# DVE's sum of a tile two units later, its statistics one unit later, and GpSimd's tile work in another order, in a language-model tower kernel

## Chip, cores and metric

The kernel runs on one core of a Trainium2 chip. The metric is the device time of one execution in microseconds (us). Of the kernel before there are three timed runs and one profiled execution. PE is the matrix engine (TensorE), PEld its weight loads, DVE is VectorE, ACT ScalarE, POOL GpSimd, SP the engine that issues plain DMAs.

## What is computed

Input are 8 sequences of 1024 tokens. Every token gets an embedding (three n-gram hashes, three gathered rows of 128, one projection). Then, with residual additions:

```
h = embed(x)                                    # 8 x 1024 x 128
y = layernorm(h)
for i in (cross, dot, cosine):                  # three attentions of width 128
    a_i = softmax(q_i k_i / s_i);  o_i = layernorm(a_i v_i) * g_i + b_i
gate = softmax([o_0, o_1, o_2] @ gw.T + gb)     # per token, 3 numbers
h = h + sum_i gate_i * o_i
y = layernorm(h);  p = softmax(y @ W_router + b_router)     # 32 experts
each expert takes its 256 most probable tokens (of 8192), applies up, silu, down
and adds p * result to h at those tokens
```

The cross attention has keys and values of half length (a convolution of stride 2). In the cosine attention q and k are divided by their norms.

## The kernel before

**Two blocks.** The first block does embedding, attention, gate and router probabilities, the second (`experts`) finds each expert's threshold bit by bit and runs the experts. The second starts when all engines have ended the first: the probabilities of the last tile are its input.

**Units and tiles.** A sequence has 8 tiles of 128 tokens. A *unit* is one tile and one attention branch, so there are 24 units in a sequence and N = 192 in all. Each engine's program (the functions under `block.tensor`, `block.vector`, `block.scalar`, `block.gpsimd`) runs one loop over `s`, 192 units and a tail of 14, written out, and each engine works through its own queue strictly in this order, with waits on semaphores. In unit `s` PE makes the scores of unit `s`, turns (transposes) the probs of `s-1` and multiplies `s-2` with the values. DVE evicts the output of `s-3` (`output`: `st` and `o`, L919 and L920), takes the row maxima of `s` (`maxima`, L913), ACT the exponent (L1078) and the copies of the turned probs into `pT` (L1087). A unit with `s % 3 == 0` is of the cross branch and has half the scores (the 512-wide maxima in the trace).

**Items.** Work for the coming sequences (gather and project tokens, keys, queries, values, the router) is cut into items, put by hand into the 24 slots of a sequence: the tables FIRST, SECOND (sequences 0 and 1), STEADY (2 to 6) and LAST (7), and DRAIN for the units after the last. Slot r of sequence b is unit 24b + r. In a slot's word, what stands before the bar is done by PE right after the scores, what stands behind it at the end of the unit; a plus means the sequence after, a minus the one before. The steady slots 14 to 16 put `v_cr` into the late part of 14 and the early part of 15, and the keys of the cosine branch, `k_c0+`, into 16. x2T (turned rows for the router) and route (router logits) are items too.

**Banks.** Items and turned probs share three PSUM banks. A little planner (before `build_program`) simulates unit times and deals the banks out; who uses a bank waits for the eviction of its last user (`release`).

**The end of a tile n** needs small steps on three engines, placed by unit:
- `tile_stats` (DVE, unit 3n+5), `tile_rstd` (POOL, 3n+5, L1187 to L1195), `tile_gate_logits` (DVE, 3n+6, L934 to L939), the exponent on ACT and `tile_gate` (DVE, 3n+7). Its last part is the chain u = h + sum over br of gate_r * o (three dependent additions, L956).
- `tile_sum` (POOL, 3n+8): z = the gated biases (L1201, L1205), then h1 = u + z (L1210), which needs DVE's chain.
- `tile_h1_stats` (DVE, 3n+9, L964 and L967), `tile_rstd2` (POOL, 3n+10, L1218 to L1223), `tile_x2` (ACT, 3n+11, L1100: the normalised row for the router).

`tile_gate` begins the chain with these lines, waiting for the buffer of two tiles before:

```
dve.wait_ge(gate_r_ok, n + 1)
if n >= 2:
    dve.wait_ge(h1_ok, n - 1)
```

**Other steps placed by unit.** DVE: `route_logits` (L858 to L863, an eviction), `route_probs` (L869 to L877) one or two units after the route item, `cos_scale` (L843 to L850: q and k times their inverse norms, two operations of 1024 columns) one unit before `k_c0`. POOL: `cos_norm` (L1177, L1180) two units before `k_c0`, `token_rstd` (L1168 to L1173), `gathers` (L1150, three indirect DMAs) four units before their gram item. In POOL's unit the order is tile_sum, tile_rstd, tile_rstd2, token_rstd and cos_norm, gathers.

Of the kernel before, what the change touches and what calls it, by code (L numbers as in the profile page):

```python
# [35 lines left out]
BR = 3  # L36
# [32 lines left out]
for _name, _width in (("ident", P), ("same", P), ("upto", P), ("after", P), ("pair", P), ("pair_below", P),  # L69
# [107 lines left out]
def build_program(nc, x_tok, emb, weights, cols, rows, consts, cand_bits, w_up, b_up, w_down, out):  # L177
    table = nc.dram_tensor("token_table", (TOK, XW), F32, kind="Internal").ap()
    with ExitStack() as ctx:
# [508 lines left out]
        def _(dve):  # L688
# [252 lines left out]
            def tile_gate(n):  # L941
# [6 lines left out]
                dve.tensor_scalar(gate[:, m, :], gate_e[:, m, :], gate_inv[:, m:m + 1], None, ALU.mult).then_inc(scale_ok, 1)  # L948
                dve.wait_ge(gate_r_ok, n + 1)
# [27 lines left out]
            for s in range(N + TAIL):  # L977
# [10 lines left out]
                if s % BR == 0 and 0 <= s - 9 < N:  # L988
                    tile_h1_stats((s - 9) // BR)
                if s % BR == 0 and 0 <= s - 6 < N:  # L990
                    tile_gate_logits((s - 6) // BR)
                if s % BR == 1 and 0 <= s - 7 < N:
                    tile_gate((s - 7) // BR)
                for where in range(2):
                    for k in PLACED.get((s - 1 - where, where), ()):
                        if ITEMS[k][0] == "route":
                            route_probs(*ITEMS[k][1:])
# [7 lines left out]
        def _(act):  # L1005
# [113 lines left out]
            for s in range(N + TAIL):  # L1119
# [8 lines left out]
                if s % BR == 2 and 0 <= s - 11 < N:  # L1128
                    tile_x2((s - 11) // BR)
# [11 lines left out]
                for k in items_at(s + 2):  # L1141
                    if ITEMS[k][0] == "xT":
                        normalise(*ITEMS[k][1:])


        @block.gpsimd
        def _(pool):
# [49 lines left out]
            def tile_sum(n):  # L1197

                m, t, b = n % 2, n % NT, n // NT
# [3 lines left out]
                for br in range(1, BR):  # L1203
                    pool.wait_ge(z_g, n * BR + br)
                    pool.tensor_tensor(zb[:, m, 0, :], zb[:, m, 0, :], zb[:, m, br, :], ALU.add).then_inc(z_g, 1)  # L1205
                pool.wait_ge(z_g, n * BR + BR)
# [44 lines left out]
            for s in range(N + TAIL):  # L1251
                if s % BR == 2 and 0 <= s - 8 < N:
                    tile_sum((s - 8) // BR)
                if s % BR == 2 and 0 <= s - 5 < N:
                    tile_rstd((s - 5) // BR)
                if s % BR == 1 and 0 <= s - 10 < N:
                    tile_rstd2((s - 10) // BR)
                for k in items_at(s + 2):
# [3 lines left out]
                    if name == "k_c" and j == 0:  # L1262
                        cos_norm(seq)
                for k in items_at(s + 4):
                    name, seq, j = ITEMS[k]
                    if name == "gram" and j < NT:
                        gathers(seq, j)

# [772 lines left out]
```

## Time and profile before

| | us |
|---|---|
| median of 3 runs | 1228.16 (1227.95 to 1229.41) |
| profiled execution | 1231.34 |
| its span, first to last instruction | 1229.6 |
| loop with full load | about 72 to 930 |
| second block from | 950.6 |

Over the span PE is busy 87%, DVE 68%, POOL 60%, ACT 55%, PEld 77%; the mean granted clock is 0.941 of full speed. The lines of a timeline give start and length in us, the engine, the line of the kernel, what is written from what, and in brackets how long the engine stood before it and which instruction ended that. A line of the waits gives who waited for whom, total us, times, and the longest. A number after x counts merged instructions.

### The profile page before, as it was taken

Reading aid. Unit: us, or ns where it says so; the run is one execution under the profiler, and the core shown is the slowest. Engines: PE = TensorE matmul, PEld = TensorE weight load, DVE = VectorE, ACT = ScalarE, POOL = GpSimd, SP = SyncE. Lnnn points to the kernel's source line nnn. Section 1 sums busy time; section 2 is a strip of 40 time slices with the busy share of each in tenths; the row PEclk is TensorE's granted clock in tenths of the full one; section 3 lists DMA queues with packets and bytes.
Section 4 is the critical chain, followed back from the end, with each engine's and each line's share of the span. In section 5 each row is a group of like instructions: output and inputs, shape, how many; then the busy total and the mean of one; then the engine's idle time right before and its main releaser. Section 6 shows DMA issues by size and latency. Waiting matters only on the chain. (4 is left out here: it accounts for less than half of the span.)

```text
span 1229.6 us, 23394 instructions
## 1 busy us (share of the span) xinstructions
PE 1065.2 (87%) x7550; PEld 944.5 (77%) x7550; DVE 830.4 (68%) x2686; ACT 677.6 (55%) x1742; POOL 736.0 (60%) x1200
## 2 busy tenths in 40 slices
PE   5689999999999999999999999999995357788672
PEld 4569888988988898998899899888884135666551
DVE  5346777787877778777777877787676777664220
ACT  0346756756676676666576666666663545434220
POOL 6356676677467547746864775353445027678885
PEclk9989999999999999999999999999997558889876
DMA  3011011010001001010100101000001103344442
GB/s 106 18 33 27 14 29 33 14 36 21 24 25 35 25 10 39 25 30 25 35 26 10 35 25 34 12 10 12 14 16 40 41 18 70 68 81 86 85 71 29
DMA packets 49085, 42.64 MB, mean 35 GB/s; under 512 B 6728, under 2 KB 44488, under 8 KB 48840
## 3 DMA queue, kind: packets, MB, share of 16 engines
q0 software_dynamic: 18432, 22.04, 9.5%
q1 hardware_dynamic: 30536, 19.13, 5.1%
q8 instruction: 62, 1.02, 0.3%
q14 instruction: 55, 0.45, 0.1%
HBM read 27.51 MB, written 13.63 MB: 33 GB/s over the span
## 5 line engine op out<-in xcount | busy, mean ns | idle before, releaser
L657 PE MATMUL mixed<-v,pT 128*128 128x131 f32 x2560 | 318.7, 276 | 3.6 <-DVE o L920 3.2
L657 PEld LDWEIGHTS mixed<-v,pT 128*128 128x128 f32 x2560 | 301.5, 190 | 5.0 <-issue 4.5
L913 DVE TENSOR_REDUCE neg_max<-scores 128x1 f32<-128x1024 f32 (+1 forms) x192 | 198.8, 1035 | 48.9 <-PE scores L444 48.8
L1150 POOL DMA_INDIRECT gram<-in_emb,ids x192 | 189.9, 989 | 64.9 <-issue 52.4
L1078 ACT ACTIVATE probs<-scores,neg_max 128x1024 f32<-128x1024 f32 (+1 forms) x192 | 186.2, 970 | 38.8 <-DVE neg_max L913 38.3
L1087 ACT ACTIVATE pT<-turned 128x512 f32<-128x512 f32 x219 | 130.0, 593 | 74.8 <-PE turned L638 73.9
L1201 POOL TENSOR_TENSOR zb<-row,gate 128x384 f32<-128x384 f32 x64 | 54.5, 851 | 144.2 <-DVE gate L948 143.8
L638 PE MATMUL turned<-con,probs 128*128 128x128 f32 x876 | 126.7, 275 | 7.6 <-ACT probs L1078 3.5
L1977 POOL DMA_INDIRECT out_h<-yw,slots x64 | 102.4, 1601 | 36.1 <-issue 20.6
L638 PEld LDWEIGHTS turned<-con,probs 128*128 128x128 f32 x876 | 101.6, 141 | 22.3 <-ACT probs L1078 8.9
L1968 POOL DMA_INDIRECT xg<-token_table,slots x64 | 64.5, 1008 | 67.6 <-DVE slots L1799 49.0
L919 DVE BATCH_NORM_STATS2 st<-mixed 128x6 f32<-128x128 f32 x192 | 56.1, 292 | 59.3 <-PE mixed L657 57.7
L442 PE MATMUL scores<-k_hi,xT_hi 128*128 128x512 f32 x192 | 82.2, 428 | 0.3 <-DVE k_lo L818 0.3
L956 DVE SCALAR_TENSOR_TENSOR u<-o,gate_r,u 128x128 f32<-128x128 f32 x128 | 78.2, 611 | 4.5
L1087 ACT ACTIVATE pT<-mixed 128x512 f32<-128x512 f32 x101 | 60.0, 594 | 30.5 <-PE mixed L638 30.0
L1908 ACT ACTIVATE hid<-scores,bup 114x256 f32<-114x256 f32 (+1 forms) x96 | 38.4, 471 | 69.3 <-PE scores L1614 69.2
L443 PE MATMUL scores<-k_lo,xT_hi 128*128 128x512 f32 x192 | 75.8, 395 | 0.0
L444 PE MATMUL scores<-k_hi,xT_lo 128*128 128x512 f32 x192 | 75.8, 395 | 0.0
L1629 PE MATMUL mixed<-wd,hid 114*128 114x128 f32 x384 | 61.4, 321 | 9.4 <-issue 9.4
L1218 POOL TENSOR_SCALAR shift<-mv 128x1 f32<-128x1 f32 x64 | 14.6, 229 | 89.4 <-DVE mv L967 87.4
L1205 POOL TENSOR_TENSOR zb<-zb 128x128 f32<-128x128 f32 x128 | 60.6, 474 | 10.0
L1629 PEld LDWEIGHTS mixed<-wd,hid 114*128 114x128 f32 x384 | 55.7, 228 | 12.5 <-issue 12.0
(350 smaller groups left out, 2550.2 us busy)
## 6 DMA issues: line engine op xcount, KB each, us to landing
wd<-in_w_down SPq DMA_DIRECT2D x32, 171.0 KB
token_table<-w SPq DMA_DIRECT2D x16, 320.0 KB, 2.4
out_h<-h SPq DMA_DIRECT2D x16, 256.0 KB, 2.3
gram<-in_emb,ids POOLq DMA_INDIRECT x192, 2.5
wu<-in_w_up SPq DMA_DIRECT2D x8, 170.5 KB, 4.0
w<-in_weights SPq DMA_DIRECT2D x1, 1174.0 KB, 6.4
xg<-token_table,slots POOLq DMA_INDIRECT x64, 3.1
out_h<-yw,slots POOLq DMA_INDIRECT x64
```

The lines of the kernel that those rows point to most:

```text
L442: pe.matmul(dst, lhs[0], rhs[0], start=first_one, stop=False)
L443: pe.matmul(dst, lhs[0], rhs[1], start=False, stop=False)
L444: return pe.matmul(dst, lhs[1], rhs[0], start=False, stop=last_one)
L638: last = pe.transpose(dst[:, j * P:(j + 1) * P], probs[:, n % 2, half * 512 + j * P:half * 512 + (j + 1) * P], ident)
L657: last = pe.matmul(mixed[:, 0:C + 3], pT[:, n % 2, j * P:(j + 1) * P], vals[:, 0:C + 3], start=(j == 0), stop=(last_half and j == half * 4 ...
L913: dve.tensor_reduce(neg_max[:, n % 4:n % 4 + 1], scores[:, (n % 2) * S:(n % 2) * S + width], AX_X, ALU.max, negate=True).then_inc(maxed, 1)
L956: last = dve.scalar_tensor_tensor(out=u[:, m, br, :], in0=o[:, n % 4, br, 0:C], scalar=gate_r[:, m, br:br + 1], in1=u[:, m, br - 1, :] if ...
L1078: act.activation(probs[:, n % 2, 0:width], scores[:, (n % 2) * S:(n % 2) * S + width], ACT.Exp, bias=neg_max[:, n % 4:n % 4 + 1], accum_ou ...
L1087: act.activation(pT[:, n % 2, half * 512:half * 512 + 512], shared_bank(TURNED_ON[n, half]), ACT.Identity).then_inc(pT_ok, 1)
L1150: pool.indirect_dma_start(gram[:, t % 4, g, :], None, emb[g], bass.IndirectOffsetOnAxis(ap=ids[:, s, t, g:g + 1], axis=0)).then_inc(gather ...
L1629: last = pe.matmul(down_bank[:, half * C:(half + 1) * C], hid[:, e % 2, c, half * P:(half + 1) * P], wd[:, e % EB, c, :], start=(c == 0), ...
L1977: pool.indirect_dma_start(rows_out, bass.IndirectOffsetOnAxis(ap=slots[:, k:k + 1], axis=0), yw[:, e % EB, half, :], None, compute_op=ALU. ...
```

## The change

Four edits.
1. DVE: the chain leaves `tile_gate` and becomes `tile_chain`, in unit 3n+9, after the gate logits of the next tile. `tile_h1_stats` moves from 3n+9 to 3n+10, behind `tile_gate`.
2. POOL: `tile_sum` keeps z; the addition becomes `tile_add` in unit 3n+9. In a unit token_rstd and cos_norm come first, then tile_rstd, tile_sum, tile_add, gathers, and tile_rstd2 last.
3. ACT: `tile_x2` goes from the start to the end of its unit, except in the units after the last.
4. The router's items stand one to three slots later, in SECOND and STEADY (and so LAST). With that the planner deals some banks otherwise.

```diff
--- before.py
+++ after.py
@@ -89,12 +89,12 @@
          "v_cr1+ | v_dc1+", "k_c0+ | gram2++", "k_c1+ | v_dc2+ v_dc3+", "x2T0 q_c0+ | v_dc4+ gram3++",
          "route0 | v_dc5+ gram4++")
 SECOND = ("v_dc6 | v_dc7", "| gram5+", "| q_c1", "xT0+ |", "gram6+ | v_dc0+", "k_d0+ | v_dc1+",
-          "gram7+ | v_dc2+", "qk_raw0+ | v_dc3+", "| gram8+", "x2T1- | qk_raw1+", "| route1-", "| gram0++", "xT1+ |",
+          "gram7+ | v_dc2+", "qk_raw0+ | v_dc3+", "| gram8+", "| qk_raw1+", "x2T1- |", "| route1- gram0++", "xT1+ |",
           "k_d1+ | qk_raw2+", "down0+ | qk_raw3+", "k_cr0+ | gram1++", "| v_cr0+", "| gram2++",
           "k_c0+ | v_cr1+", "k_c1+ | v_dc4+", "q_c0+ | gram3++", "gram4++ | v_dc5+", "x2T0 | v_dc6+", "gram5++ v_dc7+ | route0")
 STEADY = ("| xT0+", "q_c1 | ", "k_d0+ | v_dc0+", "gram6+ | v_dc1+", "qk_raw0+ | v_dc2+", "gram7+ | v_dc3+",
-          "qk_raw1+ |", "gram8+ |", "|", "x2T1- |", "xT1+ | route1-", "k_d1+ | qk_raw2+", "down0+ | qk_raw3+",
-          "k_cr0+ | ", "| v_cr0+", "v_cr1+ | gram0++", "k_c0+ | gram1++", "k_c1+ | v_dc4+", "q_c0+ | gram2++",
+          "qk_raw1+ |", "gram8+ |", "|", "|", "xT1+ | x2T1-", "k_d1+ | qk_raw2+", "down0+ | qk_raw3+",
+          "k_cr0+ | route1-", "| v_cr0+", "v_cr1+ | gram0++", "k_c0+ | gram1++", "k_c1+ | v_dc4+", "q_c0+ | gram2++",
           "gram3++ | v_dc5+", "gram4++ | v_dc6+", "x2T0 | v_dc7+", "gram5++ | route0", "|")
 
 LAST = tuple(line + extra for line, extra in zip(STEADY, ("",) * 4 + (" probT0", "", " probT1", "", " probT2") + ("",) * 15))
@@ -946,6 +946,9 @@
                 dve.scalar_tensor_tensor(out=gate_r[:, m, :], in0=gate_e[:, m, :], scalar=gate_inv[:, m:m + 1],
                                          in1=rstd[:, m, :], op0=ALU.mult, op1=ALU.mult).then_inc(gate_r_ok, 1)
                 dve.tensor_scalar(gate[:, m, :], gate_e[:, m, :], gate_inv[:, m:m + 1], None, ALU.mult).then_inc(scale_ok, 1)
+
+            def tile_chain(n):
+                m = n % 2
                 dve.wait_ge(gate_r_ok, n + 1)
                 if n >= 2:
                     dve.wait_ge(h1_ok, n - 1)
@@ -985,12 +988,14 @@
                     maxima(s)
                 for k in PLACED.get((s, 0), ()):
                     evict(k)
-                if s % BR == 0 and 0 <= s - 9 < N:
-                    tile_h1_stats((s - 9) // BR)
                 if s % BR == 0 and 0 <= s - 6 < N:
                     tile_gate_logits((s - 6) // BR)
+                if s % BR == 0 and 0 <= s - 9 < N:
+                    tile_chain((s - 9) // BR)
                 if s % BR == 1 and 0 <= s - 7 < N:
                     tile_gate((s - 7) // BR)
+                if s % BR == 1 and 0 <= s - 10 < N:
+                    tile_h1_stats((s - 10) // BR)
                 for where in range(2):
                     for k in PLACED.get((s - 1 - where, where), ()):
                         if ITEMS[k][0] == "route":
@@ -1125,7 +1130,7 @@
                     for k in PLACED.get((s - 1 - where, where), ()):
                         if ITEMS[k][0] == "route":
                             route_exp(*ITEMS[k][1:])
-                if s % BR == 2 and 0 <= s - 11 < N:
+                if s % BR == 2 and N <= s < N + 11:
                     tile_x2((s - 11) // BR)
                 for k in PLACED.get((s, 0), ()):
                     evict(k)
@@ -1141,6 +1146,8 @@
                 for k in items_at(s + 2):
                     if ITEMS[k][0] == "xT":
                         normalise(*ITEMS[k][1:])
+                if s % BR == 2 and 11 <= s < N:
+                    tile_x2((s - 11) // BR)
 
 
         @block.gpsimd
@@ -1196,13 +1203,16 @@
 
             def tile_sum(n):
 
-                m, t, b = n % 2, n % NT, n // NT
+                m = n % 2
                 pool.wait_ge(scale_ok, n + 1)
                 pool.tensor_tensor(zb[:, m, :, :], R("ln_b").rearrange("p (i c) -> p i c", c=C),
                                    gate[:, m, :].unsqueeze(2).to_broadcast([P, BR, C]), ALU.mult).then_inc(z_g, 1)
                 for br in range(1, BR):
                     pool.wait_ge(z_g, n * BR + br)
                     pool.tensor_tensor(zb[:, m, 0, :], zb[:, m, 0, :], zb[:, m, br, :], ALU.add).then_inc(z_g, 1)
+            def tile_add(n):
+
+                m, t, b = n % 2, n % NT, n // NT
                 pool.wait_ge(z_g, n * BR + BR)
                 pool.wait_ge(u_ok, n + 1)
                 if t % 4 == 0 and b > 0:
@@ -1249,22 +1259,24 @@
                     if ITEMS[k][0] == "gram":
                         gathers(*ITEMS[k][1:])
             for s in range(N + TAIL):
-                if s % BR == 2 and 0 <= s - 8 < N:
-                    tile_sum((s - 8) // BR)
-                if s % BR == 2 and 0 <= s - 5 < N:
-                    tile_rstd((s - 5) // BR)
-                if s % BR == 1 and 0 <= s - 10 < N:
-                    tile_rstd2((s - 10) // BR)
                 for k in items_at(s + 2):
                     name, seq, j = ITEMS[k]
                     if name == "xT":
                         token_rstd(seq, j)
                     if name == "k_c" and j == 0:
                         cos_norm(seq)
+                if s % BR == 2 and 0 <= s - 5 < N:
+                    tile_rstd((s - 5) // BR)
+                if s % BR == 2 and 0 <= s - 8 < N:
+                    tile_sum((s - 8) // BR)
+                if s % BR == 0 and 0 <= s - 9 < N:
+                    tile_add((s - 9) // BR)
                 for k in items_at(s + 4):
                     name, seq, j = ITEMS[k]
                     if name == "gram" and j < NT:
                         gathers(seq, j)
+                if s % BR == 1 and 0 <= s - 10 < N:
+                    tile_rstd2((s - 10) // BR)
 
         first_part.__exit__(None, None, None)
         attn.close()
```

## Rows read from the trace of the kernel before

**Rows 1.** Windows: stretch, busy us of PE, PEld, DVE, ACT, POOL; clock, DMA.
```profile
400.00:500.00 100.00, 97.83 (x726) 89.69 (x725) 75.33 (x224) 64.62 (x166) 62.61 (x114) 1.00 0.10 28
```

**Rows 2.** Waits of PE, 150 to 870 us: total us, times, longest.
```profile
PE mixed L657 <- DVE o L920: 2.6, 5, 0.5
PE turned L638 <- ACT probs L1078: 2.0, 4, 0.6
PE turned L442 <- ACT pT L1087: 1.8, 3, 0.6
PE mixed L638 <- ACT probs L1078: 1.7, 3, 0.9
PE mixed L442 <- ACT pT L1087: 0.6, 1, 0.6
```

**Rows 3.** Timeline of PE: start, length, instruction, idle time before it.
```profile
272.33 0.66 PE L638 MATMUL turned<-con,probs 128*128 128x128 f32 x4 [0.84 <-DVE h L833]
...
298.17 0.66 PE L638 MATMUL turned<-con,probs 128*128 128x128 f32 x4 [1.16 <-DVE v L823]
...
483.99 2.02 PE L657 MATMUL mixed<-v,pT 128*128 128x131 f32 x16 [0.52 <-DVE o L920]
...
506.74 0.60 PE L564 MATMUL turned<-con,w 128*128 128x128 f32 x4
```

**Rows 4.** Timeline of DVE, units of slots 12, 15 and 16.
```profile
467.72 0.28 DVE L869 TENSOR_REDUCE r_sum<-wide 128x4 f32<-128x128 f32 x1
...
468.70 0.29 DVE L919 BATCH_NORM_STATS2 st<-mixed 128x6 f32<-128x128 f32 x1
...
478.94 0.14 DVE L934 TENSOR_TENSOR logit<-o,rstd 128x9 f32<-128x9 f32 x1
...
480.45 0.25 DVE L843 RECIPROCAL inv_norm<-norm 128x16 f32<-128x16 f32 x1 [0.98 <-POOL norm L1180]
...
483.37 0.28 DVE L919 BATCH_NORM_STATS2 st<-mixed 128x6 f32<-128x128 f32 x1
```

**Rows 5.** Timeline of POOL, slots 14 and 15, and one gather.
```profile
475.24 0.19 POOL L1187 TENSOR_TENSOR sum_sq<-exp_sum 128x3 f32<-128x3 f32 x1
...
477.04 2.92 POOL L1177 TENSOR_TENSOR norm<-norm,p_half 128x16 f32<-128x16 f32 x1
480.12 0.29 POOL L1180 TENSOR_SCALAR norm<-norm 128x16 f32<-128x16 f32 x1 [0.16 <-POOL norm L1177]
...
483.44 0.94 POOL L1150 DMA_INDIRECT gram<-in_emb,ids  x1 [0.30 <-issue]
```

**Rows 6.** Timeline of DVE: the last two additions, two tiles.
```profile
457.73 1.34 DVE L956 SCALAR_TENSOR_TENSOR u<-o,gate_r,u 128x128 f32<-128x128 f32 x2
...
502.27 0.74 DVE L956 SCALAR_TENSOR_TENSOR u<-o,gate_r,u 128x128 f32<-128x128 f32 x2
```

**Rows 7.** Timeline of ACT: slots 13, 17 and 20.
```profile
473.96 0.20 ACT L1024 ACTIVATION_READ_ACCUMULATOR xn<-qk_raw 128x1 f32 x1
...
489.67 0.49 ACT L1100 ACTIVATE w<-h,shift,rstd 128x128 f32<-128x128 f32 x1 [2.13 <-POOL shift L1223]
...
506.22 0.59 ACT L1087 ACTIVATE pT<-turned 128x512 f32<-128x512 f32 x1
```

**Rows 8.** Timeline of DVE after the last product.
```profile
937.36 0.30 DVE L928 BATCH_NORM_AGGREGATE mv<-st 128x2 f32<-128x6 f32 x3
...
939.57 0.17 DVE L934 TENSOR_TENSOR logit<-o,rstd 128x9 f32<-128x9 f32 x1 [1.22 <-POOL rstd L1195]
...
943.73 0.29 DVE L964 BATCH_NORM_STATS2 st<-h 128x6 f32<-128x128 f32 x1 [0.95 <-POOL h L1210]
...
944.78 0.26 DVE L858 TENSOR_TENSOR wide<-mixed,row 128x96 f32<-128x96 f32 x1 [0.48 <-PE mixed L570]
```

**Rows 9.** Timeline of PE and ACT after the last product.
```profile
941.74 0.88 PE L564 MATMUL turned<-con,w 128*128 128x128 f32 x3 [4.61 <-ACT w L1100]
...
945.87 0.49 ACT L1100 ACTIVATE w<-h,shift,rstd 128x128 f32<-128x128 f32 x1
```

## Prediction, made before the result was known

> **What bounds the kernel now.** I read the busy time by windows first. In a window of the loop the matrix engine is busy 97.8 of 100 us, DVE 75, ACT 65, POOL 63, at the full granted clock, 2.4 GHz [rows 1]. What DVE can gain is thus worth only what it takes from the 2.2 us of every 100 in which PE stands. Then the waits of PE name those 2.2 us [rows 2]: 2.6 us for `o` (five times 0.52), 2.4 us (1.8 and 0.6) for a pT copy, 3.7 us (2.0 and 1.7) for a probs. The timeline places them: the wait for `o` is in slot 16 of sequences 2 to 6, the pT waits in slot 17 (four times 0.6), the waits for probs in slot 0 and in the last sequence. Two more, in sequence 1, wait for `h` and `v` of DVE, 0.84 and 1.16 us [rows 3]. Nothing else in the loop is open to a gain. After the last product, whose statistics DVE aggregates at 937.36 [rows 8], the order is another: the tail of tile 63 is one serial chain of DVE, POOL, ACT and PE, and every microsecond in it is one of the time.
>
> The profiled execution took 1231.34 us (span 1229.6), 3.2 us above the median 1228.16; the sum is made against it and carried to the median.
>
> **Slots 15 and 16, the largest term.** Today DVE ends slot 15 with the scaling of q and k: logits from 478.94, a wait of 0.98 us for POOL's norm, scaling from 480.45, next `st` at 483.37, so 2.92 us of scaling [rows 4]. PE's product waits for the `o` just behind it, 0.52 us [rows 3]. The change puts into that same unit, ahead of the scaling, two more things: the chain of three additions (slot 15 is a multiple of 3) and `route_probs`, since route1 now stands second in slot 13 and its probabilities come two units later.
> - POOL: the norm now stands before the tile's rstd. It can start when the last square is read, 474.16 [rows 7], and takes 477.04 to 480.41, 3.37 us; the rstd takes 475.24 to 477.04, 1.8 us [rows 5]. The moved statistics of the tile before come first: DVE's would be ready about 473.1 by its place in slot 13, and from such statistics to the x2 that needs POOL's four pass some 1.5 us (943.73 + 0.6 to 945.87 [rows 8, 9]). So the norm starts at 474.6, ends at 478.0, and rstd is there at 479.8 instead of 477.0. DVE, at the logits today at 478.94, now stands for it.
> - DVE from 479.8: logits 0.5, chain, `route_probs` 0.98 (467.72 to 468.70), scaling 2.92 [rows 4].
> - The chain's first addition starts 0.37 us before the second; the other two take 1.34 us in the one tile and 0.74 in the other [rows 6]: 1.7 or 1.1 us. POOL forms z right after rstd, so here I take the slow one.
> The end is 479.8 + 0.5 + 1.7 + 0.98 + 2.92 = 485.9, 2.5 us later than 483.37. But x2T and route leave slots 9 and 10, 0.4 and 0.8 us of PE work, and return only in slots 10 and 13, so PE and what follows it (squares, keys) run 0.8 us early up to slot 13: 1.8 us remain, all on PE, since `o` is what it waits for already. Bounds: 1.2 with the fast chain, 2.5 without the early slots; 0.5 less than nothing if the gap closed. Taken 1.8, five sequences: **+9.0**.
>
> What decides between 1.7 and 1.1 for a chain is who reads beside it: both tiles' rows have the same operands [rows 6]. The Trainium skill ("SBUF — State Buffer", Who interferes with whom) says that a DVE instruction with two SBUF inputs is shut out while a GpSimd instruction that reads SBUF holds the shared port, for the whole of it. By that rule a chain that z no longer accompanies costs 1.1 everywhere; were POOL done with z when the chain starts in slot 15, the sum would be 3.0 us lower.
>
> **Slot 17, a gain.** ACT stands 2.13 us at 489.67 for POOL's shift, with k_hi and a pT behind it [rows 7]; x2 moves to the end of the unit, behind both, and PE's 0.6 us go. Four times: **-2.4**. What is late next is that same x2: POOL's shift now stands behind the gathers of slots 14, 15 and 16 (three each, 0.94 + 0.30 us [rows 5]), at about 494.5 to 495 by adding them up from rstd; ACT reaches x2 about 494 and holds q_hi and the next pT for some 0.8 us, of which PE has 0.5 in hand: 0.3 us, five times, **+1.5** (from 0 to 1.5 us each).
>
> **Slot 0, a gain.** DVE's maximum of slot 23 comes late because the chain stands in slot 22. It loses 1.7 and gets 0.5 of statistics. All waits for probs, 3.7 us [rows 2]: **-3.7**.
>
> **Sequence 1.** The 0.84 us for `h` follow a slowed scaling with z beside it, which is now elsewhere; at 298.17 the planner gives the transposes another bank, freed by gram5 and not by v_dc7, one eviction and 0.9 us earlier [rows 3]. **-1.8**, from 0 to -2.5.
>
> **Slot 21, a new wait.** x2T0 is PE's first item there, at 506.74 [rows 3], and needs the x2 of unit 20. x2 was the first thing of ACT's unit 20 and is now the last, after the pT at 506.22 + 0.59 [rows 7]; its 0.49 us end at 507.2. PE stands 0.5 us, in six sequences (2 to 7): **+3.0** (0 to 0.6 each).
>
> **After the last product.** Statistics of DVE are there at 937.66, POOL's rstd today only at 939.5, because z of tile 62 stood before it [rows 8]. With the new order: rstd 938.9, logits 0.6, then the chain of tile 62, 1.7, ahead of gate 63 (941.7), then the statistics of 62 to 942.3, POOL's four of them to 943.8 and only then z of 63, because POOL's queue has them in this order; x2 of 62 at 944.3. From x2T (941.74 [rows 9]) to DVE's route logits (944.78 [rows 8]) are 3.0 us, now 944.35 to 947.4; the statistics of tile 63 stand behind this eviction (0.8 us), at 948.2 instead of 943.73. Everything after, x2 at 945.87 [rows 9] first, moves by that: **+4.4**. Low bound 1 (rstd earlier, only the queue of POOL counts), high 5.5.
>
> Edits at nothing: the gate stays where it is, `tile_add` is POOL's own successor of z and its buffer is written two tiles later; the other maxima wait for their scores, as the idle 25 us of DVE in 100 show [rows 1]. If that cover went, 1.1 us a tile would show.
>
> **Sum:** 9.0 - 2.4 + 1.5 - 3.7 - 1.8 + 3.0 + 4.4 = +10.0 us: 1241.3 in a profile like this one, **1238.2** as median. From the bounds of its terms it lies between 1231 and 1245.
>
> **Rivals.** (a) Faster. The norm, now first on POOL, is there before DVE needs it, so the 0.98 us wait of slot 15 pays for the chain. That decides if rstd comes by 478.5, for which the squares would have to come 1.3 us early, not 0.8; and if z is over. Then slot 16's 2.6 us go too: -2.6 - 2.4 - 3.7 - 1.8 + 4.4 - (nothing at slot 21) = -6.1, 1222.0. For it speaks that DVE's work is spread better over the three units; against it, that slot 15 holds three long pieces. Chance 0.13. The Trainium skill ("Perfetto Trace Analysis", Identifying the Most-Contended Engine) holds the matmul share to be a bad measure of headroom and the weight loads' share a good one; that is 89.7 here and would leave room for more than 2.2 us in 100, but the trace has no wait behind it.
> (b) No change. The overrun of slot 15 is half (0.9 x 5), slot 21 and the end too (1.5 and 2.2), the gains whole: +4.5 - 7.9 + 1.5 + 2.2 = +0.3, 1228.5. Chance 0.10.
> (c) Worse. POOL, with the norm, the rstd, z and nine gathers in three units, is so late that x2 holds ACT 1.5 us in slot 18, not 0.3: +6.0 more, 1244, and up to 1248. Against it: PE is itself later by then. Chance 0.15.
> My forecast keeps 0.62.
>
> **Chances.** 0.2%, 2.5 us, is about what a measurement here tells from no change. Slower by more than that: the forecast, (c): 0.77. Within: (b), 0.10. Faster: (a), 0.13. The range 1227.5 to 1246 leaves out (a) and the top of (c).
>
> **What would show it.** Right: PE's wait for `o` in slot 16 grows from 0.5 to 2 us and more, DVE's wait on POOL's rstd appears in slot 15, that for the norm vanishes; the waits at slots 0 and 17 vanish; PE waits for ACT's x2 0.5 us in slot 21; the second block starts over 4 us later after the last product. Wrong: `o` waits of 0.5 us or less in slot 16, no wait at slot 21, or statistics of tile 63 within 8 us of the last product's end.

## The result, and the profile after

The changed kernel takes **1241.71 us** (median of 4 runs, 1240.82 to 1245.38), the kernel before 1228.06 on the same chip: a ratio of 1.0114 (95% interval 1.0094 to 1.0135), slower. The profiled execution took 1240.82 us, span 1239.0, 9.5 us over that of before. The forecast was 1241.3 in a profile like that and 1238.2 as a median.

Where the 9.5 us lie, from the starts of PE's scores in the two traces (before, after, in us): up to the first unit 2.6 less; sequence 0, 115.6 and 114.3; **sequence 1, 112.8 and 118.2**; sequence 2, 109.0 and 110.7; sequences 3 to 5, 109.3 and 109.5 on average; sequence 6, 103.7 and 104.7; sequence 7, 95.9 and 95.3; **from the last product to the second block, 13.7 and 19.0**; the second block 0.1 more. Sequences 3 to 5 thus pay almost nothing, against all that the forecast puts there. The median moved more than the traces, by 13.65 us: the profiled execution of the changed kernel was the fastest of its four, that of the kernel before slower than all four runs of it.

PE's waits between 150 and 870 us of the changed kernel, the view of [rows 2]:

```profile
PE turned L558 <- DVE qk_raw L850: 5.6, 3, 2.0
PE mixed L558 <- DVE qk_raw L850: 3.3, 2, 1.7
PE mixed L657 <- DVE o L920: 2.4, 5, 0.5
PE turned L638 <- DVE h L833: 2.1, 1, 2.1
PE turned L638 <- ACT pT L1092: 1.8, 1, 1.8
PE mixed L564 <- ACT w L1105: 1.5, 3, 0.7
```

Five waits for the scaling of q and k (8.9 us) stand in slot 16, where the kernel before had one of 0.2 us; the waits for `o` stay at 0.5 us each; the waits for probs and those of slot 17 are gone. PE is busy 97.29 of the 100 us from 400, where it was 97.8 [rows 1].

Slot 15 on DVE, the answer to [rows 4], and POOL beside it [rows 5]:

```profile
480.87 0.79 DVE L934 TENSOR_TENSOR logit<-o,rstd 128x9 f32<-128x9 f32 x1 [0.46 <-POOL rstd L1202]
...
481.97 0.35 DVE L959 SCALAR_TENSOR_TENSOR u<-o,gate_r,h 128x128 f32<-128x128 f32 x1
482.36 0.88 DVE L959 SCALAR_TENSOR_TENSOR u<-o,gate_r,u 128x128 f32<-128x128 f32 x2
483.15 0.28 DVE L869 TENSOR_REDUCE r_sum<-wide 128x4 f32<-128x128 f32 x1
...
484.09 0.24 DVE L843 RECIPROCAL inv_norm<-norm 128x16 f32<-128x16 f32 x1
...
486.91 0.29 DVE L919 BATCH_NORM_STATS2 st<-mixed 128x6 f32<-128x128 f32 x1
```
```profile
475.69 2.91 POOL L1184 TENSOR_TENSOR norm<-norm,p_half 128x16 f32<-128x16 f32 x1
...
479.95 0.88 POOL L1202 TENSOR_TENSOR rstd<-var_eps,m_half 128x3 f32<-128x3 f32 x1
480.80 0.83 POOL L1208 TENSOR_TENSOR zb<-row,gate 128x384 f32<-128x384 f32 x1
```

The norm is over at 479.0, and DVE stands for rstd, which POOL forms behind it. Then come logits (1.10 us up to the chain), chain (1.18), probabilities (0.94) and scaling (2.82): 6.0 us in a row. PE stands 1.66 us at the turning of the keys (`k_c0+`, the first item of slot 16, which reads the scaled rows) and 0.47 us for `o` at the product behind it, where it stood 0.52 in all [rows 3]:

```profile
486.01 0.63 PE L558 MATMUL turned<-con,qk_raw 128*128 128x128 f32 x4 [1.66 <-DVE qk_raw L850]
...
487.54 2.03 PE L657 MATMUL mixed<-v,pT 128*128 128x131 f32 x16 [0.47 <-DVE o L920]
```

Two things were not foreseen. The first is in sequence 1, on POOL and on ACT, and then on PE (units 26 and 27):

```profile
188.06 0.46 POOL L1220 TENSOR_TENSOR h<-u,zb 128x128 f32<-128x128 f32 x1 [5.50 <-DVE u L959]
188.75 1.09 POOL L1157 DMA_INDIRECT gram<-in_emb,ids  x1 [0.24 <-issue]
...
192.43 0.23 POOL L1175 TENSOR_SCALAR shift<-mv 128x4 f32<-128x4 f32 x1
```
```profile
194.40 0.88 ACT L1097 ACTIVATE xn<-h,shift,rstd 128x128 f32<-128x128 f32 x2 [2.42 <-POOL shift L1180]
```
```profile
196.85 0.66 PE L558 MATMUL mixed<-con,qk_raw 128*128 128x128 f32 x4 [1.09 <-DVE h L833]
...
200.46 0.63 PE L638 MATMUL turned<-con,probs 128*128 128x128 f32 x4 [1.80 <-ACT pT L1092]
202.03 0.87 PE L638 MATMUL mixed<-con,probs 128*128 128x128 f32 x4 [0.94 <-DVE q_lo L813]
```

POOL's addition waits in its queue 5.5 us for a chain that now comes two units later; the gathers and the tokens' statistics stand behind it. Later in the same sequence, in unit 42, PE stands 2.09 us for `h`. x2, now ahead of the copy of gramT on ACT, waits for POOL's shift, and POOL is late because two small operations take 0.99 and 1.06 us beside DVE's scaling (268.29 to 270.57), for 0.23 and 0.21 us elsewhere:

```profile
268.62 0.99 POOL L1228 TENSOR_SCALAR shift<-mv 128x1 f32<-128x1 f32 x1
269.67 1.06 POOL L1229 TENSOR_SCALAR ve<-mv 128x1 f32<-128x1 f32 x1
```
```profile
271.69 0.49 ACT L1105 ACTIVATE w<-h,shift,rstd 128x128 f32<-128x128 f32 x1 [2.14 <-POOL shift L1233]
```

The second is PE's clock. Windows of the changed kernel (length, PE's busy time, granted clock, DMA share, GB/s): behind the stall of sequence 1, in slot 16 of sequence 2, and in slot 16 of sequence 3.

```profile
202.00:205.00 3.00, 2.97 (x15) 0.55 0.19 46
...
375.00:380.00 5.00, 4.53 (x25) 0.66 0.23 59
```
```profile
486.00:489.00 3.00, 2.52 (x21) 1.00 0.23 57
```

Three times in the loop, from 202.3, 274.0 and 376.4 us, the clock is granted at half, 1.2 GHz, for 3.4 us; in the trace of before it is at 2.4 GHz in all three places. Slots 16 of sequences 2 and 3 have the same 1.66 + 0.47 us of stall and last 9.23 and 7.62 us: **1.6 us for one such stretch**. At that price the three make some 4.8 of the 9.5 us, an estimate from this one pair.

### The profile page after: what moved, and what is told of

Same layout as the page of the kernel before. It is cut to its first block and busy times, and to the rows that moved or that the text cites. A ratio compares the mean times of both kernels' runs of the same rounds, so it can differ in the third digit from the quotient of the medians.

```text
span 1239.0 us, 23392 instructions
## 1 busy us (share of the span) xinstructions
PE 1062.0 (86%) x7548; PEld 944.8 (76%) x7550; DVE 816.0 (66%) x2686; ACT 671.7 (54%) x1742; POOL 728.3 (59%) x1200
## 5 line engine op out<-in xcount | busy, mean ns | idle before, releaser
L657 PE MATMUL mixed<-v,pT 128*128 128x131 f32 x2560 | 322.5, 278 | 3.0 <-DVE o L920 3.0
L657 PEld LDWEIGHTS mixed<-v,pT 128*128 128x128 f32 x2560 | 305.2, 192 | 4.2 <-issue 4.2
L1092 ACT ACTIVATE pT<-turned 128x512 f32<-128x512 f32 x212 | 126.0, 595 | 63.0 <-PE turned L638 62.8
L638 PE MATMUL turned<-con,probs 128*128 128x128 f32 x848 | 120.8, 274 | 6.7 <-DVE h L833 2.1
L638 PEld LDWEIGHTS turned<-con,probs 128*128 128x128 f32 x848 | 98.1, 141 | 19.2 <-ACT probs L1083 9.7
L1220 POOL TENSOR_TENSOR h<-u,zb 128x128 f32<-128x128 f32 x64 | 29.9, 466 | 110.9 <-DVE u L959 88.6
L1092 ACT ACTIVATE pT<-mixed 128x512 f32<-128x512 f32 x108 | 64.4, 596 | 47.9 <-PE mixed L638 47.8
L638 PE MATMUL mixed<-con,probs 128*128 128x128 f32 x432 | 65.4, 274 | 1.4 <-DVE q_lo L813 0.9
L1874 ACT ACTIVATE below_a<-odd,cand 128x448 bf16<-128x448 f32 x58 | 38.8, 669 | 44.6 <-DVE cand L1720 42.9
```

The costliest lines, as they stand in the source:

```text
L638: last = pe.transpose(dst[:, j * P:(j + 1) * P], probs[:, n % 2, half * 512 + j * P:half * 512 + (j + 1) * P], ident)
L657: last = pe.matmul(mixed[:, 0:C + 3], pT[:, n % 2, j * P:(j + 1) * P], vals[:, 0:C + 3], start=(j == 0), stop=(last_half and j == half * 4 ...
L1092: act.activation(pT[:, n % 2, half * 512:half * 512 + 512], shared_bank(TURNED_ON[n, half]), ACT.Identity).then_inc(pT_ok, 1)
```

## The experiments

The runs come in three groups, each on a chip of its own, with the kernel before run beside it; its median is given with the group, and a ratio is to that median. The changed kernel itself was not run again in any group.

### First group: one part of the loss at a time (before: 1229.79 us)

**u_chain14.** The chain of slot 15 alone goes one unit forward.

```diff
+                if s % UNITS == 14 and s < N:
+                    tile_chain((s - 8) // BR)
-                if s % BR == 0 and 0 <= s - 9 < N:
+                if s % BR == 0 and s % UNITS != 15 and 0 <= s - 9 < N:
                     tile_chain((s - 9) // BR)
```

> The changed kernel with one edit: in slot 15 alone the chain of three additions is issued one unit earlier (slot 14), so slot 15 holds logits, route_probs and the scaling, without the chain. Theory (the chain is the larger part of slot 15's overrun): PE's gaps in slot 16 fall from 2.1 us to 0.5 to 1.0 us in each of five sequences, and no half-clock stretch follows there; time 6 to 8 us lower, 1234 to 1236. Rival (POOL's rstd, now behind the norm, sets DVE's time in slot 15): DVE waits 1.5 us or more for rstd instead of 0.46, the gaps shrink by 0.5 us at most, time at most 3 us lower, 1239 or more.

Measured: 1238.96 us, ratio 1.0065 (1.0042 to 1.0087). Slot 16 and slot 18 on PE, and ACT ahead of the latter:

```profile
484.53 0.63 PE L558 MATMUL turned<-con,qk_raw 128*128 128x128 f32 x4 [0.54 <-DVE qk_raw L850]
```
```profile
497.40 0.38 PE L506 MATMUL turned<-w,gramT 128*128 128x128 f32 x1 [0.54 <-ACT pT L1094]
```
```profile
495.89 0.49 ACT L1107 ACTIVATE w<-h,shift,rstd 128x128 f32<-128x128 f32 x1 [2.25 <-POOL shift L1235]
```

The gap falls by 1.1 us, as much as the chain takes; DVE's wait for rstd stays at 0.46 us. The half-clock stretch of sequence 2 is gone. Half of it comes back in slot 18: PE, now earlier, meets the pT held by the late x2. So the theory has the mechanism right. The ratio is 0.5 points under the changed kernel's 1.0114, some 6 us and so the low end of the 6 to 8 us expected; the time itself is 3 us above the forecast.

**u_addlast.** POOL adds behind the gathers of its unit.

```diff
-                if s % BR == 0 and 0 <= s - 9 < N:
-                    tile_add((s - 9) // BR)
                 for k in items_at(s + 4):
...
                         gathers(seq, j)
+                if s % BR == 0 and 0 <= s - 9 < N:
+                    tile_add((s - 9) // BR)
```

> The changed kernel with one edit: POOL's addition u + z of a tile is issued behind the gathers of its unit instead of before them. Theory (in sequence 1 POOL stands 5.5 us for DVE's u with gathers and the tokens' statistics queued behind, and this makes PE's stalls of 1.1, 1.8 and 0.9 us in units 26 and 27 and the half-clock stretch behind them): those stalls fall to below 1.0 us in sum, sequence 1 is 3 to 5 us shorter, 1237 to 1239. Rival (the stalls come from DVE's own place of the work, not from POOL's queue): sequence 1 as before the edit within 1 us, 1241 to 1242.

Measured: 1245.11 us, ratio 1.0109 (1.0076 to 1.0142). Sequence 1 is 114.0 us instead of 118.2, the 1.1 us gap of unit 26 and the half-clock stretch of unit 27 gone, 1.5 us of the others left (the kernel before has 1.1 there): this shows the cause of 4.2 of the 5.4 us of sequence 1. Unit 42 keeps its 2.09 us and its stretch. The time is not lower for other reasons. Slot 20 of sequence 0 is 1.5 us longer (the addition behind three gathers lets DVE wait 1.35 us with its statistics, and the scaling of q and k stands behind them, so PE waits 1.55 us for 0.95); sequence 5 has a half-clock stretch; and the trace reached the first unit 2.6 us later than the changed kernel's.

```profile
168.34 0.63 PE L558 MATMUL mixed<-con,qk_raw 128*128 128x128 f32 x4 [1.55 <-DVE qk_raw L850]
```

**u_drain.** The tail in the old order from unit 193. The edit also puts the statistics ahead of the gate in their unit all through the loop, which the forecast below leaves out.

```diff
+                if s % BR == 0 and s > N and s - 9 < N:
+                    tile_h1_stats((s - 9) // BR)
                 if s % BR == 0 and 0 <= s - 6 < N:
                     tile_gate_logits((s - 6) // BR)
-                if s % BR == 0 and 0 <= s - 9 < N:
+                if s % BR == 0 and 0 <= s - 9 and s <= N:
                     tile_chain((s - 9) // BR)
+                if s % BR == 1 and 0 <= s - 10 and s <= N + 1:
+                    tile_h1_stats((s - 10) // BR)
                 if s % BR == 1 and 0 <= s - 7 < N:
                     tile_gate((s - 7) // BR)
-                if s % BR == 1 and 0 <= s - 10 < N:
-                    tile_h1_stats((s - 10) // BR)
+                    if s > N:
+                        tile_chain((s - 7) // BR)
...
                     tile_sum((s - 8) // BR)
-                if s % BR == 0 and 0 <= s - 9 < N:
+                    if s > N:
+                        tile_add((s - 8) // BR)
+                if s % BR == 0 and 0 <= s - 9 and s <= N:
                     tile_add((s - 9) // BR)
```

> The changed kernel with one edit: from unit 193 on (the tail after the last scores) the chain stands again behind its gate, the statistics of a tile one unit earlier and POOL adds behind its z; the rstd stays ahead of z. Theory (the serial tail pays for the moved chain and statistics): from the last product to the second block 18.97 us become 12 to 14, nothing else moves, time 5 to 7 us lower, 1235 to 1237. Rival (the tail is set by route and x2T of the last tiles, not by chain and statistics): 17 us or more stay, time within 2 us of the changed kernel's.

Measured: 1236.49 us, ratio 1.0050 (1.0036 to 1.0065), but the tail takes 16.15 us, not 12 to 14; the rest came from the loop, and in this trace 1.5 us from an earlier first unit. In the loop the earlier statistics bring POOL's queue (rstd2, norm, rstd) forward, DVE no longer stands at the logits, and slot 16's gap is 1.2 us in three sequences instead of 1.66 (1.8 and 1.5 in sequences 5 and 6):

```profile
476.76 0.79 DVE L934 TENSOR_TENSOR logit<-o,rstd 128x9 f32<-128x9 f32 x1
```

So what sets the start of slot 15's work is a queue that begins with the statistics two units before. And with no wait for rstd at all a gap of 1.2 us stays: that much goes with the serial work on DVE.

**u_dve_pool.** Chain, statistics and POOL's order as before; x2 at the end and the items in their new slots remain.

> The changed kernel with DVE's chain and statistics and POOL's order put back as in the kernel before; left are x2 at the end of its unit and the router's items in their new slots. Theory (the loss is in the chain's and POOL's part): 1225 to 1229, that is the kernel before, plus 0.5 us in slot 21 of six sequences, less 0.6 us in slot 17 of four and 1 us in unit 47. Rival (the late x2 holds ACT and then PE): 1231 to 1235, with waits of PE for x2 in slot 21 of 1 us or for pT in slots 18 and 19.

Measured: 1233.98 us, ratio 1.0034 (1.0020 to 1.0049): the rival, though its wait in slot 21 is 0.7 us and not 1. A steady sequence is 0.5 to 1.0 us longer than before: slot 17's gap is gone, but x2T waits for x2 in slot 21, and slot 9, from which x2T has left, shows a wait for probs that it used to cover.

```profile
503.92 0.30 PE L564 MATMUL turned<-con,w 128*128 128x128 f32 x1 [0.71 <-ACT w L1100]
```
```profile
555.80 0.44 PE L638 MATMUL turned<-con,probs 128*128 128x128 f32 x2 [0.50 <-ACT probs L1078]
```

### Second group: the clock, x2's place, and a mended version (before: 1229.07 us)

**b_stall.** The kernel before, with DVE made late in slot 15.

```diff
+        pad_v = asb("pad_v", [P, 8, 8, BR])
...
                     if name == "k_c" and j == 0:
+                        if seq > 2:
+                            for j2 in range({3: 4, 4: 5, 5: 6, 6: 7, 7: 8}[seq]):
+                                dve.tensor_reduce(pad_v[:, seq, j2, :], gain[:], AX_X, ALU.add)
                         cos_scale(seq)
```

> The kernel before with dummy reductions (128x393 each, into a scratch tile) on DVE ahead of the scaling of q and k in slot 15 of sequences 2 to 6: 4, 5, 6, 7 and 8 of them. They make PE's stall in slot 16 longer, about 1.2 us in sequence 2 up to 3 us in sequence 6, and nothing else of the change is there. Theory (the granted clock halves for 3.4 us in a loop that is otherwise full when PE stands some 1.7 us or more, and that costs 1.6 us on top): half-clock stretches behind the long stalls of the later sequences, none behind the first, and those slots longer by the stall and 1.6 us. Rival (the half-clock stretches of the changed kernel come from elsewhere): no stretch behind any of them, each slot longer by its stall alone.

Measured: 1233.85 us, ratio 1.0043 (1.0026 to 1.0060). The waits for the scaling are 0.71, 1.10, 1.27, 2.05 and 2.51 us in sequences 2 to 6. Windows around the last two (PE, PEld, DVE, ACT, POOL, then the clock):

```profile
698.00:708.00 10.00, 7.47 (x59) 6.91 (x59) 9.61 (x25) 4.71 (x9) 8.02 (x11) 1.00 0.15 39
809.00:819.00 10.00, 7.75 (x49) 7.12 (x50) 9.39 (x22) 4.14 (x8) 3.72 (x8) 0.83 0.09 28
```

The stall of 2.51 us is followed by half clock and its sequence is 3.6 us longer; that of 2.05 us is not, and its sequence is 0.95 us longer. One stretch thus follows a stall alone, with nothing else of the change there; it is one case, and the theory's 1.7 us is not a boundary, since 2.05 us had none. And in sequence 3 slot 16 is 1.25 us longer but slot 17 **0.85 shorter** with x2 at its old place (its pT is ready once PE is late); the added stall costs 0.4 us. So slot 17's gap can be had only once, by x2's new place or by being late.

**u_x2.** The changed kernel with x2 at the start of its unit.

```diff
-                if s % BR == 2 and N <= s < N + 11:
+                if s % BR == 2 and 0 <= s - 11 < N:
                     tile_x2((s - 11) // BR)
...
-                if s % BR == 2 and 11 <= s < N:
-                    tile_x2((s - 11) // BR)
```

> The changed kernel with x2 at the start of its unit on ACT, as before. Theory (the later statistics and POOL's order make x2's shift come late in slot 17, about 4 us after ACT would ask for it, with k_hi and pT behind it): the 0.41 us gaps of slot 21 go, but PE stands 2 to 4 us more in slot 17 or 18, time 1250 to 1262; x2's new place is then a condition of the other edits. Rival (x2 at the start finds its shift ready as before but for slot 17's old 0.6 us): 1240 to 1243.

Measured: 1265.76 us, ratio 1.0287 (1.0259 to 1.0316). ACT stands 5.14 us for the shift, PE 3.58 in slot 17: the theory, at a time 4 us above its range. x2's new place is a condition of the rest.

```profile
507.24 0.49 ACT L1105 ACTIVATE w<-h,shift,rstd 128x128 f32<-128x128 f32 x1 [5.14 <-POOL shift L1231]
```

**c14_drain_x2late.** u_chain14, u_drain (with its earlier statistics in the whole loop) with POOL's old order in the tail too, and x2 of slot 17 one unit later. The lines for the last:

```diff
-                if s % BR == 2 and 11 <= s < N:
+                if s % BR == 2 and 11 <= s < N and s % UNITS != 17:
                     tile_x2((s - 11) // BR)
+                if s % UNITS == 18 and s < N:
+                    tile_x2((s - 12) // BR)
```

> The changed kernel with three edits together: slot 15's chain in slot 14; the tail (from unit 193) in the order of the kernel before on DVE and POOL, statistics of a tile ahead of the gate of their unit; and the x2 of slot 17 issued at the end of unit 18 instead of unit 17. Theory (in slot 18 ACT stands for POOL's shift with the pT behind it, 0.54 us of PE once slot 16 is mended, and the same wait holds gramT in unit 42): the slot 18 gaps of 0.54 us and most of the 2.1 us of unit 42 go with its half-clock stretch, the tail is back at 13.7 us, time 1226 to 1230. Rival (the late x2 comes late for something else): a gap of over 0.5 us at x2T in slots 21 or 10, or a POOL wait for x2, time 1231 to 1234.

Measured: 1227.21 us, ratio 0.9981 (0.9967 to 0.9996). Slot 18's gap and 1.5 of the 2.1 us of unit 42 are gone, with its half-clock stretch, but slots 20 and 21 of that sequence are 0.7 us longer each. Sequences 2 to 5 last 107.8 to 108.9 us, where the kernel before has 109.0 to 109.4. The tail is at 15.1 us. What the earlier statistics give in it was not taken apart.

**best1.** The same with x2T0 in the second half of its unit (`"| x2T0 v_dc7+"`) and POOL's addition behind the gathers in sequence 1 alone.

> The one before with two more edits: x2T of slot 21 in the second half of its unit, and in sequence 1 alone POOL's addition behind the gathers. Theory (the 0.41 us of slot 21 and the stalls and half-clock stretch of units 26 and 27 are the last losses of the change): 6 x 0.4 and 4 us lower than the one before, 1220 to 1224, faster than both kernels. Rival (x2T in the second half delays the router's item and route's probabilities, the bank of the planner moves and a pT waits): no lower than the one before less 4.

Measured: **1220.56 us, ratio 0.9928 (0.9901 to 0.9955)**, with no half-clock stretch in the loop past the first units, like the kernel before. From 400 to 500 us (the sum row of that window):

```profile
sum 100.00, PE 99.25 PEld 91.50 DVE 77.33 ACT 66.34 POOL 65.64; mean PE 99.25 PEld 91.50 DVE 77.33 ACT 66.34 POOL 65.64
```

PE is at 99.25 of 100, and sequences 2 to 7 are 1.4 to 2.0 us shorter each than before.

### Third group (before: 1248.07 us)

This chip runs the kernel before itself 19 us slower, and in three of the four traces engines stand for releasers that the trace can't name ("remote"), which no other trace shows between 100 and 900 us. These four traces also lack the landings of the gathers, which all others have, so part of it can be a hole of the trace. One in best2:

```profile
500.57 0.60 ACT L1019 ACTIVATE k_hi<-mixed 128x512 fp32r<-128x512 f32 x1 [3.87 <-remote]
```

Only local readings are taken from it. The changed kernel was not run on this chip, so how much of a loss here is the edit's and how much the chip's can't be told from the ratio.

**u_pool.** POOL's order as before, the addition ahead of rstd.

> The changed kernel with POOL's order as before (z first, then rstd, then the tile's second rstd, then the tokens' statistics, the norm and the gathers); the addition stands in its new unit, behind z. Theory (in slot 15 DVE stands for rstd because the norm was put ahead of it, and in unit 42 ACT stands for a shift queued behind gathers): PE's gap of 1.66 us in slot 16 falls to 0.5 to 1.0 us in each of five sequences and the 2.1 us of unit 42 to about 1 us, with their half-clock stretches gone; time 1232 to 1236. Rival (POOL's second rstd now waits in its unit for the statistics of DVE, with the norm and the gathers behind it, and the norm comes later than DVE wants it): DVE stands for the norm in slot 15, the gap stays at 1.5 us or more, time 1240 to 1246.

Measured: 1305.18 us, ratio 1.0446 (1.0397 to 1.0495). Each had a part. Slot 16's gap falls to 0.4 us in sequences 2 to 4 and 0.74 in the next two, as in the theory. But, as in the rival, POOL asks for the statistics ahead of DVE's issue of them and stands up to 6.4 us, rstd and the tokens' statistics behind it, and PE pays in other slots: against the changed kernel's trace slot 0 is 2.2 to 4.0 and slot 10 2.2 to 3.9 us longer in each of sequences 2 to 6.

```profile
482.40 0.24 POOL L1228 TENSOR_SCALAR shift<-mv 128x1 f32<-128x1 f32 x1 [4.07 <-DVE mv L970]
```
```profile
521.64 0.63 PE L558 MATMUL turned<-con,qk_raw 128*128 128x128 f32 x4 [0.43 <-DVE qk_raw L850]
```

POOL's new order is thus needed by the later statistics, though slot 16 alone is better off with the old one.

**u_tables.** The router's items in their old slots.

> The changed kernel with the router's items in their old slots (x2T1 first in slot 9, route1 second in slot 10), so its probabilities leave slot 15. Theory (route_probs is 1 us of slot 15's overrun, and the late x2 makes x2T1 wait): the gap of slot 16 falls from 1.66 to about 0.7 us, a new gap of some 0.5 us stands at x2T1 in slot 9, time 2 to 4 us lower, 1238 to 1240. Rival (POOL's rstd and the chain set slot 15, and probabilities only fill a wait): the slot 16 gap over 1.3 us, time 1242 to 1245.

Measured: 1297.81 us, ratio 1.0384 (1.0337 to 1.0432). In slot 9 PE stands 2.58 us for x2, not 0.5. And without probabilities in slot 15 its gap stays at 1.63 us or more, the rival's side: DVE waits 0.9 us longer for rstd.

```profile
592.12 0.53 PE L564 MATMUL turned<-con,w 128*128 128x128 f32 x2 [2.58 <-ACT w L1105]
```
```profile
504.47 0.79 DVE L934 TENSOR_TENSOR logit<-o,rstd 128x9 f32<-128x9 f32 x1 [1.36 <-POOL rstd L1202]
```

From slot 11 on PE reaches slot 15 0.9 us earlier when route is not in slot 13, but POOL's queue does not. In slot 17 PE stands another 2.1 to 2.8 us for a pT in sequences 2 to 5, which neither theory nor rival has.

**b_x2.** The kernel before with slot 17's x2 (sequences 2 to 6) at the end of its unit.

> The kernel before with one edit: in slot 17 of sequences 2 to 6 x2 stands at the end of its unit on ACT, behind k_hi and the copy of pT. Theory (0.59 us of PE and the small gaps beside it are all that the wait for POOL's shift costs): slot 17 is 4.04 us long instead of 4.89, nothing else moves, time 3 to 4 us lower, 1225 to 1226. Rival (slot 16's wait for o hides the same time, or slot 18 gives it back): within 1 us of before.

Measured: 1252.99 us, ratio 1.0020 (0.9992 to 1.0048). One of its ten runs took 3117.79 us. Inconclusive: sequences 2 to 5 are 2.5 to 2.8 us longer in this trace than in before's on the other chip, with waits in slots 13, 14, 17 and 18 that neither theory has.

**best2.** best1 with the tail's old order from tile 61 on.

> The kernel best1 with the tail's old order (chain behind its gate, statistics one unit earlier, POOL's addition behind z) already from tile 61 on instead of 62. Theory (POOL's second rstd of tile 61 holds z of tile 62 by 1.4 us in the tail): 15.12 us from the last product to the second block become 13.7, time 1 to 1.5 us lower, 1219 to 1220, and 0.7 to 0.9 per cent below the kernel before. Rival (the tail is set by something else): 15 us stay.

Measured: from the last product to the second block 13.76 us, as forecast. But the time is 1253.25 us, ratio 1.0025 (0.9999 to 1.0051), with k_hi late by up to 4.6 us behind "remote" waits and PE standing up to 3.8 us in slot 17 for the pT behind it. The gain of best1 is thus shown on one chip and absent, in nearly the same kernel, on another; why is open.

## Why the prediction was right, and where it was not

Time, sign and range held, but the sum came right by errors that cancel. Forecast and measured in the traces: sequences 2 to 7, +7.4 and +2.7; sequence 1, -1.8 and +5.4; after the last product, +4.4 and +5.2; ahead of sequence 1, nothing and -3.9. So +10.0 against 9.5 is in good part luck, and the median lies 3.5 us above its forecast. By the forecast's own signs, one stands on the wrong side: PE's waits for `o` in slot 16 did not grow (0.47 us, under the 0.5 named as wrong). The stall grew by the forecast amount, but at the turning of the keys ahead of the product, a reader of the scaled rows that the forecast passed over. Term by term:

- **Slots 15 and 16, +9.0.** Measured: stall of 2.13 us for 0.52 in sequences 2 to 4 (2.43 for 0.52 and 2.46 for 0.67 in the next two), +8.5 us in all, and 1.6 more for the half-clock stretch. The working held: POOL's rstd sets DVE, then 6.0 us of serial work (forecast 6.1). In that sum two errors cancel: the logits took 1.10 for 0.5, the chain 1.18 for 1.7. The early slots save less than they seem to, since POOL's queue isn't early with PE (u_tables).
- **The chain at 1.7 or 1.1 us.** The slow value was taken, with z beside it in slot 15; it took 1.18. After the change no chain of 64 has more than 0.89 us for its last two additions, where 50 had over 1.2; one addition takes 369 ns on average instead of 611:

```profile
L956 DVE SCALAR_TENSOR_TENSOR u<-o,gate_r,u 128x128 f32<-128x128 f32 x128 | 78.2, 611 | 4.5
```
```profile
L959 DVE SCALAR_TENSOR_TENSOR u<-o,gate_r,u 128x128 f32<-128x128 f32 x128 | 47.2, 369 | 4.5
L934 DVE TENSOR_TENSOR logit<-o,rstd 128x9 f32<-128x9 f32 x64 | 19.4, 303 | 8.8 <-POOL rstd L1202 8.8
```

  What z meets now is the 9-element product of the logits, 0.79 us in slot 15 instead of 0.14. The rule of the Trainium skill ("SBUF — State Buffer", Who interferes with whom), that such an instruction is shut out for as long as POOL's holds the port, agrees: 0.79 is about the length of z's first product (0.83). It is not borne out in full by what follows: z's two additions run from 481.71 to 482.70 beside the chain and cost it only 0.14 us (0.88 for 0.74). The 31 us less in the chains (14 less in DVE's whole busy time) bought nothing in slot 16, where PE waits.
- **Slot 17, -2.4.** The gap went, and with small ones behind it slot 17 is 0.85 us shorter in four sequences. But b_stall shows that the delay of slot 16 alone takes it away.
- **ACT held by x2, +1.5.** Wrong in its place: ACT waits for the shift (1.13 us at 496.23), but PE is late by slot 16's stall and does not. Once that is mended, 0.54 us appear (u_chain14).
- **Slot 0 and probs, -3.7.** As forecast; no wait for probs is left among the rows.
- **Slots 9, 10 and 13.** Costed at nothing but work moved: they give another 0.55 us a sequence. Where from is in part open: u_dve_pool, which has the chain in its old place and the items in the new ones, keeps waits for probs of 0.50 and 0.26 us in slots 9 and 10 that the changed kernel does not have.
- **Sequence 1, -1.8.** The term that failed: +5.4. The bank of unit 47 gave its 1.0 us. What was missed was "`tile_add` is POOL's own successor of z", listed at nothing: it stands a unit further, waits up to 5.5 us for DVE's chain, and the queue behind it (three gathers, four operations of token statistics) was not walked for the sequence where the tokens' statistics fall into that unit. In unit 42 x2 at the end of the unit before holds gramT: PE stands 2.1 us, where it stood 1.3 in all, and POOL's two slowed operations are in that wait; the 0.84 us that the forecast takes as gained are not. Two half-clock stretches follow, by the price above 3.2 us of it.
- **Slot 21, +3.0.** PE stands 0.41 us in sequences 2 to 5, 0.67 in sequence 6 and 1.05 in sequence 7, 3.4 us in all; by length the slots are 0.59 to 0.63 and, in sequence 7, 1.1 us longer, +4.1.
- **After the last product, +4.4.** Measured +5.2. The mechanism is in the rows as written: POOL forms z of tile 63 last, and the statistics of tile 63 stand behind the wait for x2T [rows 8].

```profile
952.28 0.26 DVE L858 TENSOR_TENSOR wide<-turned,row 128x96 f32<-128x96 f32 x1 [4.42 <-PE turned L570]
...
953.03 0.28 DVE L967 BATCH_NORM_STATS2 st<-h 128x6 f32<-128x128 f32 x1
```

  best2 gives it all back.

Rival (a) fell, but not by its condition on rstd. Its 480.8 can't be held against the 478.5 named there, since slot 15 of that sequence starts 1.9 us later in this trace and slot 9 2.4: carried over it came at 479.0 or 478.5, late by little or nothing. What felled the rival is z, which was not over, and the serial work: in u_drain DVE waits for no rstd and the gap is still 1.2 us. Rival (c) fell as well: a pT held by x2 stopped PE nowhere in slot 18 of sequences 2 to 6. The rule of the Trainium skill ("Perfetto Trace Analysis", Identifying the Most-Contended Engine) on the weight loads' share would have left headroom. No run shows that this share bound anything: best1 has 91.50 us of weight loads and 99.25 us of matmuls in 100, and what it gained in the loop, 1.4 us in 100, came out of the 2.2 that the matmul share had left.

## What to carry to other kernels

When an operation moves a unit later, walk every in-order queue that waits for it, in each phase of the schedule, the irregular first sequences too: the price was in what stood behind one addition of POOL, and in the tail. A stall's cost is not its length: where the engine has another wait a little further on, 1.25 us more in one slot cost 0.4 (b_stall), and gains and losses of neighbouring slots must not be added. A good move of work can lose as a whole and win with two or three of its placements mended, so look at each slot before the change is given up, and measure the winner on more than one chip.

## What the runs showed of the hardware

PE's granted clock falls from 2.4 to 1.2 GHz inside a loop that is otherwise full, behind or in one stall. In the ten traces outside the third group, from unit 4 to 188, stalls of 0.6 to 1.6 us (43; of stalls within 5 us of each other the longest counts) were never followed by it, of 1.65 to 2.3 us (26) 13 times, of 2.5 to 3.6 us (7) 6 times. One stretch lasts 3.4 us, in three places of u_x2 6.8, and 3.4 us cost 1.6 (one pair of slots). Stalls of equal length, 1.66 us in slot 16 of sequences 2, 3 and 4, had it once in three: the length of the stall alone does not decide it, and what else does is open. Whether such stalls make the time vary more from run to run is not shown: the changed kernel varied by 4.6 us over 4 runs, the kernel before by 2.5 over 4 and by 6.5 over the 18 of the first group.
